# A gated cross-attention and LoRA block on one Trainium2 core: the program written anew, tile by tile

## What is computed

```python
def fake_quant(x, scale, zp):
    q = clip(round(x / scale + zp), 0, 255)
    return (q - zp) * scale
x = x + tanh(g_xattn) * (fake_quant(layernorm(x), s1, z1) @ fake_quant(ctx, s2, z2))   # per batch
h = layernorm(x)
logits = h @ Wr.T                              # 4 experts, the best 2 are kept
gates = softmax(logits of the best 2, else 0)
mid = einsum('tf,erf->ter', h, A)              # A: 4 experts x rank 16 x 2048
delta = sum_e gates[e] * (mid[e] @ B[e].T) * 4
x = x + tanh(g_ffn) * delta
```

## Time and profile before

| | |
|---|---|
| time, median of 3 runs | 423.1 us (422.08 to 425.37) |
| profiled execution | 423.39 us, span 421.7 us |
| TensorE matmul busy | 355.9 us, 84% of the span |
| VectorE busy | 314.9 us, 75% |
| ScalarE busy | 260.8 us, 62% |
| POOL busy | 85.6 us, 20% |
| HBM read, written | 51.42 MB, 16.78 MB |

### The profile page before, as it was taken

How to read it: one execution, slowest core, us unless ns; L and a number is a source line. 1 busy time by engine, 2 the same in 40 slices (tenths; PEclk the granted TensorE clock), 3 DMA queues, 4 the chain that set the end, 5 groups by cost and what they waited for, 6 DMA issues and landing times. The chain is left out here.

```text
span 421.7 us, 7130 instructions
## 1 busy us (share of the span) xinstructions
PE 355.9 (84%) x2352; PEld 207.1 (49%) x2352; DVE 314.9 (75%) x732; ACT 260.8 (62%) x240; POOL 85.6 (20%) x74
## 2 busy tenths in 40 slices
PE   0075569489898999989898999999999999999974
PEld 0032324265545454645555565656565656565552
DVE  2469994889877878787878777777777777676684
ACT  1757796578868585868777465656555565656150
POOL 1000000222222040403122222222313231314030
PEclk9999759779999999999999999999999999999986
DMA  4999980269474645465552322222322222312022
GB/s 143 331 400 426 427 371 2 99 209 307 185 234 133 210 145 189 181 184 173 195 203 101 100 103 101 99 99 99 99 99 99 99 99 99 102 50 101 0 101 100
DMA packets 22240, 68.51 MB, mean 162 GB/s; under 512 B 3204, under 2 KB 3716, under 8 KB 20100
## 3 DMA queue, kind: packets, MB, share of 16 engines
q1 hardware_dynamic: 22216, 68.20, 45.3%
HBM read 51.42 MB, written 16.78 MB: 162 GB/s over the span
## 5 line engine op out<-in xcount | busy, mean ns | idle before, releaser
L538 PE MATMUL ps_main<-q,q1T 128*128 128x512 f16 x928 | 212.1, 379 | 0.0
L538 PEld LDWEIGHTS ps_main<-q,q1T 128*128 128x128 f16 x928 | 87.7, 98 | 101.0 <-issue 7.0
L404 ACT ACTIVATE h_hi<-x,small_tile 128x1024 f16<-128x1024 f32 x32 | 39.4, 1233 | 61.6 <-DVE small_tile L825 61.6
L350 POOL TENSOR_TENSOR h_lo<-work,h_hi 128x1024 f16<-128x1024 f32 x31 | 66.7, 2151 | 46.1 <-ACT work L408 44.3
L809 DVE SCALAR_TENSOR_TENSOR x<-ps_main,small_tile,xt 128x512 f32<-128x512 f32 x60 | 44.7, 746 | 24.2 <-DMA out_x<-x 14.8
L787 DVE BATCH_NORM_STATS2 small_tile<-xt 128x6 f32<-128x512 f32 x64 | 40.7, 682 | 19.8 <-DMA xt<-in_x 19.8
L344 POOL TENSOR_TENSOR small_tile<-small_tile 128x1 f32<-128x1 f32 x16 | 8.8, 551 | 200.8 <-DVE small_tile L821 200.8
L390 ACT ACTIVATE x_byte<-xt,small_tile 128x1024 uint8<-128x1024 f32 x32 | 38.1, 1233 | 16.2 <-DVE small_tile L803 16.2
L814 DVE BATCH_NORM_STATS2 small_tile<-x 128x6 f32<-128x512 f32 x64 | 44.3, 692 | 1.7
L883 DVE TENSOR_TENSOR x<-ps_delta,x 128x512 f32<-128x512 f32 x64 | 42.3, 683 | 2.7 <-PE ps_delta L604 2.7
L383 ACT ACTIVATE ctx_stage<-ctx_stage,small_tile 128x1024 uint8<-128x1024 f32 x32 | 38.7, 1233 | 3.4 <-DMA ctx_stage<-in_ctx 3.4
(11 more groups left out here) (97 smaller groups left out, 367.8 us busy)
## 6 DMA issues: line engine op xcount, KB each, us to landing
xt<-in_x SPq DMA_DIRECT2D x32, 512.0 KB, 3.8
q<-in_ctx SPq DMA_DIRECT2D x16, 1024.0 KB, 18.0
ctx_stage<-in_ctx SPq DMA_DIRECT2D x32, 512.0 KB, 5.4
out_x<-x SPq DMA_DIRECT2D x64, 256.0 KB, 2.2
x<-in_L_ffn_A SPq DMA_DIRECT2D x1, 512.0 KB
x<-in_L_ffn_B SPq DMA_DIRECT2D x1, 512.0 KB, 14.9
small_tile<-in_L_xattn_x_scale SPq DMA_DIRECT2D x2, 0.5 KB, 4.0
small_tile<-in_L_xattn_x_zp SPq DMA_DIRECT2D x2, 0.5 KB, 4.3
```

The lines of the kernel that those rows point to most:

```text
L350: nc.gpsimd.tensor_tensor(h_lo[:, h, :], work[:, h, :], h_hi[:, h, :], ALU.subtract).then_inc(h_lo_ready, 1)
L404: nc.scalar.activation(h_hi[:, h, :], x1[:, b % 2, half(h)], ACT.Identity, bias=h_bias[:, :], scale=h_rstd[:, :]).then_inc(h_hi_ready, 1)
L538: mm = pe.matmul(acc[:, :], q1T[:, b % 2, k, :], q2[:, batch(b), k, cols(n)], start=(k == 0), stop=(k == KT - 1))
```

## The change

The same mathematics in a program written anew. In words:

- The host lays out A (one 128 x 1088 float32 array, turned) and B (128 x 2048, doubled), and joins six parameters in one array, which ScalarE's queue loads. The turning of A and B on TensorE and their splits in the load stage are gone. A gets a power-of-two scale per column (`largest_of_a`, `scales_of_a`, `powers_of_a`, `spread_scales`, `copy_scales`) and is split on POOL into two float16 parts in place of three bfloat16 ones, so that `mid_hi` has 136 columns and `mid_lo` 68; `rank_gates` multiplies the middle by the scales. `high_of_b` and `low_of_b` write B's two halves on VectorE.
- x lies in a ring of four tiles and x1 is written in place; loads of x wait for the store of four tiles before.
- In the load stage each row is added to four banks of tile 0 and, from row 4 on, to three of tile 1 (with the first four caught up). The tiles' scales and q1T of tiles 0 and 1 have new places; q1T of these two is copied on VectorE.
- Rows of batch 1 come whole, in two stages: rows 0 to 3 ahead of slot 4, then three per slot in slots 4 to 7. B's array lies in stage 1 first, A's in the x ring's fourth place.
- q1 is turned through the bank of the gates and copied at once (2048 columns); `scale_x` and `high_part` are one operation of 2048 columns; stores are 512 KB but for the last tile's.
- Both delta pairs of tile b-2 are in slot b; for the last tile the four banks are separate. Nothing is a loop any more.

The diff, cut to its core (buffers and banks; SyncE; POOL; ScalarE's order; TensorE; VectorE's order):

```diff
-        xt = sb("xt", [P, 2, D], F32)
-        x1 = sb("x1", [P, 2, D], F32)
+        xr = sb("xr", [P, RING, D], F32)
+        ctx_stage = sb("ctx_stage", [P, STAGES, N], F32)
         q1T = sb("q1T", [P, 2, KT, P], F16)
         lora_bT = sb("lora_bT", [P, N], F32R)
-        a_parts = sb("a_parts", [P, KT, 3, J], BF16)
+        a_parts = sb("a_parts", [P, KT, 2, J], F16)
...
+        first_banks = [ps_main + ps_delta, [ps_mid] + ps_turn + [ps_main[0]],
+                       [ps_main[1], ps_delta[0], ps_delta[1], ps_main[0]]]
         def product_bank(b, n):
...
+            def load_ctx(k):
+                wait(sp, ctx_coded, k - STAGES + 1)
+                if k == 1:
+                    sp.wait_ge(b_ready, 1)
+                sp.dma_start(ctx_stage[:, k % STAGES, :], ctx_pairs[(KT + k) // 2, k % 2, :, :]).then_inc(ctx_loaded[k % STAGES], 16)
...
+            load_x(0)
+            load_row(0)
+            load_row(1)
+            load_x(1)
+            for k in range(2, 12):
+                load_row(k)
+            load_x(2)
+            for k in range(12, KT):
+                load_row(k)
+            sp.dma_start(a_raw, lora_a).then_inc(a_loaded, 16)
+            sp.dma_start(b_raw, lora_b).then_inc(b_loaded, 16)
+            load_ctx(0)
+            sp.wait_ge(a_ready, 1)
+            load_x(3)
+            load_ctx(1)
+            load_ctx(2)
...
+            c = 3
+            for b in range(3, TILES):
+                if b == 3:
+                    store(0, range(2), HALF)
+                    load_x(4)
+                    todo = 2
+                elif b == 4:
+                    store(1, range(2), HALF)
+                    load_x(5)
+                    load_ctx(c)
+                    c += 1
+                    store(2, range(2), HALF)
+                    load_x(6)
+                    todo = 2
+                else:
+                    store(b - 2, range(2), HALF)
+                    if b + 2 < TILES:
+                        load_x(b + 2)
+                    todo = 3
+                for _ in range(todo):
+                    if c < KT:
+                        load_ctx(c)
+                        c += 1
+            store(LAST - 1, range(2), HALF)
+            store(LAST, range(NB), BANK)
...
+            def split_a():
+                a_view = a_raw.rearrange("p (k j) -> p k j", j=J)
+                pool.wait_ge(a_loaded, 16)
+                pool.wait_ge(a_scale_ready, 1)
+                nc.gpsimd.tensor_tensor(a_view, a_view, scales[:, 1, :].unsqueeze(1).to_broadcast([P, KT, J]), ALU.mult).then_inc(a_part_step, 1)
+                pool.wait_ge(a_part_step, 1)
+                nc.gpsimd.tensor_copy(a_parts[:, :, 0, :], a_view).then_inc(a_part_step, 1)
+                pool.wait_ge(a_part_step, 2)
+                nc.gpsimd.tensor_tensor(a_parts[:, :, 1, :], a_view, a_parts[:, :, 0, :], ALU.subtract).then_inc(a_ready, 1)
+            power_x(0)
+            power_x(1)
+            power_x(2)
+            split_a()
+            power_h(0)
+            low_part(0, 0)
+            power_h(1)
+            low_part(0, 1)
+            power_x(3)
...
+            scale_x(0)
+            scale_row(0)
+            scale_row(1)
+            scale_row(2)
+            scale_x(1)
+            for k in range(3, 13):
                 scale_row(k)
...
+            scale_x(2)
+            scale_row(13)
+            scale_row(14)
+            scale_row(15)
+            copy_q1T(2)
...
+            scale_ctx(1)
+            copy_loT(0)
...
+            scale_x(3)
+            high_part(1)
+            normal_half(1, 0)
+            normal_half(1, 1)
+            copy_q1T(3)
...
+            copy_hiT(2, 1)
+            scale_ctx(3)
+            copy_loT(2)
+            scale_x(4)
+            gate_exp(2)
+            copy_q1T(4)
+            c = 4
+            for b in range(4, TILES):
+                high_part(b - 1)
+                normal_half(b - 1, 0)
+                normal_half(b - 1, 1)
+                if c < KT:
+                    scale_ctx(c)
+                    c += 1
+                copy_hiT(b - 1, 0)
+                copy_hiT(b - 1, 1)
+                if b < LAST:
+                    scale_x(b + 1)
+                copy_loT(b - 1)
+                if b < LAST:
+                    copy_q1T(b + 1)
+                if c < KT:
+                    scale_ctx(c)
+                    c += 1
+                gate_exp(b - 1)
+                if c < KT:
+                    scale_ctx(c)
+                    c += 1
+            high_part(LAST)
+            copy_hiT(LAST, 0)
+            copy_hiT(LAST, 1)
+            copy_loT(LAST)
+            gate_exp(LAST)
...
+                    mm = pe.matmul(ps_mid[:, J:2 * J], hT[:, h, k, :], a_parts[:, kk, 0, :], start=False, stop=(kk == KT - 1))
...
+            def last_delta():
+                pe.wait_ge(gT_step, TILES)
+                pe.wait_ge(x1_ready, NB * TILES)
+                pe.wait_ge(out_ready, NB * LAST)
+                banks = ps_delta + ps_main
+                for n in range(2):
+                    pe.matmul(banks[n][:, :], gT_hi[:, :], lora_bT[:, cols(n)], start=True, stop=False)
+                pe.wait_ge(gT_ready, TILES)
+                for n in range(2):
+                    pe.matmul(banks[n][:, :], gT_lo[:, :], lora_bT[:, cols(n)], start=False, stop=True).then_inc(delta_done, 1)
+                for n in range(2, NB):
+                    pe.matmul(banks[n][:, :], gT_hi[:, :], lora_bT[:, cols(n)], start=True, stop=False)
+                    pe.matmul(banks[n][:, :], gT_lo[:, :], lora_bT[:, cols(n)], start=False, stop=True).then_inc(delta_done, 1)
...
+                for k in range(KT):
+                    if k == JOIN - 1:
+                        turn_q1(1, 0)
+                    if k == KT - 2:
+                        turn_q1(2, 0)
+                    pe.wait_ge(row_coded, k + 1)
+                    for n in range(NB):
+                        product(0, n, k, general)
+                    if k == JOIN:
+                        pe.wait_ge(q1T_ready, 2)
+                        for kk in range(k):
+                            for n in range(3):
+                                product(1, n, kk, general)
+                    if k >= JOIN:
+                        for n in range(3):
+                            product(1, n, k, general)
+                main(1, 3, general)
+                scales_of_a()
+                main(2, 0, general, 0, 8)
+                spread_scales()
+                main(2, 0, general, 8)
+                main(2, 1, general)
+                turn_hi(0)
+                main(2, 2, general, 0, 10)
+                high_and_turn_low(0)
+                main(2, 2, general, 10)
+                low(0)
+                main(2, 3, general, 0, 14)
+                turn_gate(0, 3)
+                main(2, 3, general, 14)
+                turn_q1(3, 1)
+                turn_hi(1)
+                main(3, 0, general, 0, 4)
+                delta(0, 0)
+                main(3, 0, general, 4)
+                delta(0, 2)
+                high_and_turn_low(1)
+                main(3, 1, general, 0, 8)
+                low(1)
+                main(3, 1, general, 8)
+                turn_hi(2)
+                main(3, 2, general, 0, 10)
+                turn_gate(1, 4)
+                high_and_turn_low(2)
+                main(3, 2, general, 10)
+                low(2)
+                main(3, 3, general, 0, 8)
+                delta(1, 0)
+                main(3, 3, general, 8, 14)
+                turn_gate(2, 4)
+                main(3, 3, general, 14)
+                delta(1, 2)
+                turn_q1(4, 3)
+                for b in range(4, TILES):
+                    if b == 4:
+                        main(b, 0, general)
+                        delta(b - 2, 0)
+                        main(b, 1, general)
+                        delta(b - 2, 2)
                     else:
+                        main(b, 0, general, 0, 4)
+                        delta(b - 2, 0)
+                        main(b, 0, general, 4)
+                        delta(b - 2, 2)
+                        main(b, 1, general)
+                    turn_hi(b - 1)
+                    main(b, 2, general, 0, 10)
+                    high_and_turn_low(b - 1)
+                    main(b, 2, general, 10)
+                    if b < LAST:
+                        turn_q1(b + 1, b - 1)
+                    low(b - 1)
+                    main(b, 3, general, 0, 14)
+                    turn_gate(b - 1, min(b + 2, TILES))
+                    main(b, 3, general, 14)
+                delta(LAST - 1, 0)
+                delta(LAST - 1, 2)
+                turn_hi(LAST)
+                high_and_turn_low(LAST)
+                low(LAST)
+                turn_gate(LAST, TILES)
+                last_delta()
...
+            def largest_of_a():
+                dve.wait_ge(a_loaded, 16)
```

(93 more changed lines are left out.)

1039 lines of the change are left out of this document (418 added, 621 removed).

## The result

The changed kernel takes **453.22 us** (median of 4 runs, 450.71 to 456.28); the kernel before, run beside it, 423.73 (422.08 to 425.37). Ratio 1.0699, 95% interval 1.062 to 1.0779: 7.0% slower. The prediction said 437.0 (413 to 449), slower at 0.70. The direction was right, the size was not: the time lies 4 us above the range. The profiled execution has a span of 451.6.

What follows compares the result with a forecast made beforehand. It took in-order engine queues to bound the kernel up to slot 7, then gapless TensorE: 147.7 to main(4,0), 105 for slots 4 to 7, 161.6 for slots 8 to 15, tail 21.9, sum 436.2, 437.9 with 1.7 outside; it said 437 (413 to 449).

Steps and rivals of the forecast that it cites:

- main(4,0) starts: Load stage through tile 3: main(4,0) starts at 147.7, where it was 142.3, so 5.4 later.
- slots 4 to 7: Slots with three whole rows each: 26 a slot, 27 for slot 4, 105 against 91.1, 13.9 more.
- slots 8 to 15: Slots without context rows: narrower middles bring 20.7 to 20.2 a slot, 161.6 in all, 3.8 less.
- tail: After main(15,3): 22.8 becomes 21.9, by 0.9 more for h_hi, 1.3 less for deltas, 0.5 less for middles.
- Load stage: First stage: row 15 coded at 62, 4.6 earlier; TensorE done at 63.5, not 73.06, with one bank more.
- the four chains: Load to loop: scaling A, bias_h(0) 78; load_ctx(1), low(0) 96.8; q1T(3), main(3,0) 114; tile 3, main(4,0) 147.7.
- the first two chains: Before the loop: A's scaling and POOL split to bias_h(0) at 78; B's split and load_ctx(1) to low(0) at 96.8.
- 25.1 at least: Slots 4 to 7: floor per slot of the chain through copy_q1T, second scale_ctx, code_ctx and gates, against 22.8.
- rival C: Slots 4 to 7: waits drop TensorE to 1.2 GHz, moving turn_q1 some 1.7; slots 27.7, total 447; chance 0.15.
- its 0.4: Slots 8 to 15: stats_h and the low part put the gate 0.4 past the fourteen matmuls that cover it.
- A: Whole kernel, faster: VectorE's work the only bound after the load, main(4,0) at 127, slots 25.1; 412.6; chance 0.14.
- B: Whole kernel, gains and losses cancel: chains some 5 shorter, main(4,0) at 142.3, slots 25.1; 425.5; chance 0.16.

Runs made afterwards that it cites:

- e4: Changed kernel with POOL computing power_h(0) ahead of the three operations that split A; 450.66 us, ratio 1.0619.
- e8: Changed kernel with ScalarE doing copy_loT(0) and gate_exp(0) ahead of scale_ctx(1), before the loop; 448.94 us, ratio 1.0597.
- e10: Changed kernel with high_of_b and low_of_b ahead of bias_h(0) in VectorE's queue; 449.01 us, ratio 1.0574.
- e14: The spread row order of e13 together with the edits of e3, e8 and e4; 422.92 us, ratio 1.0008.
- e15: On top of e14, the work on tiles 1 and 3 ahead of the loop ordered anew; 413.85 us, ratio 0.9758.
- experiment 2: Changed kernel with 22 added matmuls keeping TensorE busy before turn_gate in slots 4 to 7; 452.47 us, ratio 1.0642.
- e5: Changed kernel with SyncE issuing a slot's first context row ahead of the store and x load; 449.88 us, ratio 1.0578.
- e1: Changed kernel with VectorE's second code_ctx behind weigh instead of ahead of add_main(b,2), slots 4 to 7; 444.31 us, ratio 1.0464.
- e13: Against e9, a slot's three rows spread evenly over SyncE's, ScalarE's and VectorE's queues; 433.36 us, ratio 1.0241.
- e3: Changed kernel with add_delta(14,1) ahead of bias_h(15) in the tail; 449.97 us, ratio 1.0603.
- e17: On top of e15, SyncE issues a slot's third row between the store and the x load; 410.19 us, ratio 0.9674.
- e7: On top of e6, ScalarE does the exponential ahead of its second scale_ctx; 441.56 us, ratio 1.0407.
- e9: Changed kernel with two codings a slot deferred to the next, ScalarE's rows and exponential reordered, two rows issued before the store; 447.24 us, ratio 1.0529.
- run 31: Not a follow-up run: the words come from the sentence that float16 matmuls with 68 moving columns run 31 ns apart.
- e12: Changed kernel with the row order of e9 and the edits of e3, e8 and e4; 434.05 us, ratio 1.0234.
- e6: Changed kernel with the edits of e1 and e5 together; 437.47 us, ratio 1.0312.
- experiment 11: The experiment that ran e17: third row issued ahead of the x load, on top of e15; 410.19 us, ratio 0.9674.

## Why the prediction fell short

**The ledger.** Its four terms against the profiled execution:

| | predicted | measured | |
|---|---|---|---|
| main(4,0) starts | 147.7 | 154.08 | +6.4 |
| slots 4 to 7 | 105 | 113.7 | +8.7 |
| slots 8 to 15 | 161.6 | 158.2 | -3.4 |
| tail | 21.9 | 25.7 | +3.8 |
| span | 436.2 | 451.6 | +15.4 |

Every step went the way it was forecast in direction (head later, slots 4 to 7 the largest loss, slots 8 to 15 a gain), except the tail.

**Load stage: each small term a little low.** Parameters landed at 7.10, not 5.5; ScalarE's two standstills were 7.7 and 4.6, not 7 and 4.2. Row 15 was coded at 64.85 instead of 62, and TensorE was through with the rows, at the start of main(1,3), at 68.09 instead of 63.5. That is still ahead of the 73.06 of the earlier trace rows, with one bank more, so the regime was right. The gap of some 7 between constants and TensorE's program held (12.2 to 18.98).

**Head: the four chains were right, three durations weren't.** largest_of_a took 2.09 (said 1.2), high_of_b 2.34 (said 1.6), low_of_b 3.85 (said 2.5, bound 3.0). bias_h(0) came at 81.18 with VectorE idle 5.35 before it (said 78, some 6); low(0) at 100.64 after 7.93 (said 96.8, 8). POOL's split_a took 2.49 + 1.09 + 2.26 = 5.8, at the low end. The two B steps were not underpriced as work: both began while a POOL operation was running, and from that operation's end they took 1.1 and 2.15, less than the 1.6 and 2.5 of the forecast (see the last section). What the sum had at nothing is 1.3 and 1.7 of waiting beside POOL. Of the 6.4 by which main(4,0) came late, some 3 were there at the end of the load stage, 3.8 at low(0) and 4.3 at main(3,0) (118.28, said 114); tile 3 took 35.8 in place of 33.7. e4, e8 and e10 take the first two chains apart: 4.1, 5.2 and 7.5 at gate 0. The two waits themselves (6 and 8) were right, but e14 and e15 show what the forecast did not see: once they are gone, gates 0 to 3 still take 72 until, in one edit, x3's scale and tile 1's h are taken ahead of the gates of tile 0, and then 62. It read chains one at a time.

**Slots 4 to 7: the step that failed.** The prediction put it: "DMA is no bound: 3 rows, an x tile and a store, 5.2 MB in 25 us". It priced the chain at "25.1 at least", took 26 and, for slot 4, 27, and put two terms at nothing: the wait for a row's landing, and the low clock behind TensorE's wait, which it kept for rival C. Slot 6 shows both. From gate to gate (208.66 to 237.46) it took 28.8, and 25.1 + 2.03 (ScalarE's wait for the row at 230.56) + 1.8 (the clock, as in experiment 2) is 28.9. The bytes were right and the conclusion wrong: SyncE's queue is in order, so the row's load stood 11.9 behind the freeing of its stage. e5 bears the sum out: with its issue moved the landing waits are gone and the slots take 27.0 to 27.2, where 25.1 + 1.8 is 26.9. In the four slots the landings are 3.3 of the 8.7, and three slots at 26.9 in place of 26 another 2.7. Slot 4 was 28.8 long (154.08 to 182.9), not 27: its main(4,0) too ran in large part at the low clock, 4.95 from its start to the delta (154.08 to 159.03) where 3.46 is the full rate. The last 0.9 is not taken apart. The named chain (second scale_ctx behind copy_q1T, coding ahead of rank_gates) was real, as e1 and e13 show.

**Slots 8 to 15: mid_lo.** The prediction granted 0.16 a tile of a possible 0.48, since weight loads might set the pace. At 343.31 sixteen mid_lo start within 0.50, 31 ns apart, where before sixteen took 0.96: all of it was gained. The gate stayed covered, so its 0.4 was not lost. 158.2 / 8 = 19.8 a slot in place of 20.2 lies at the low end of the bounds, 19.7 to 20.8. The Trainium skill (TensorE: Matmul & The Clock Gate, Back-to-back issue gap) gives N / 2.4 + 2.5 ns for one isolated matmul, by which 68 columns are an estimated 30.8, and says that a stream with weight loads sustains about 81 ns at 128 columns. The first agrees with the 31 here. The second does not: eight transposes of 128 columns with eight loads start within 343.31 - 342.86 = 0.45, 56 ns each.

**Tail: a wait not seen.** The forecast costed the tail by durations and asked for each new order only what it saves. At 434.43 TensorE stood 4.95 for add_delta(14,1), with turn_hi(15) behind it at 435.88; e3 gave 2.4 back. Asking "what is queued behind this wait" once more would have found it.

**The rivals.** A (412.6, faster) did not happen. e17 comes near its number, 410.2, but by luck: main(4,0) starts at 137.6 there (A: 127), and the four slots take 227.18 - 137.56 = 89.6 (A: 100.4), two errors that cancel. What e17 does show is that VectorE, ScalarE and two stages are no bound at 25.1 a slot. B was missed by the same late chains. C came nearest: its mechanism is there, 1.8 a slot against the 1.7 that it gave, and its 151 + 111 for head and slots stands against 154.1 + 113.7. The argument against it, that the clock had stayed full in slots 3 to 7 of before, failed because TensorE's waits before the gates there were 0.2 and not 5 to 7.

## What to carry to other kernels

A queue taken in order turns *where an operation stands* into a cost of its own: the same instructions cost 451.6 and 409.1 here, and the span moved by 20.3 with the places of three rows and one exponential. Put work that comes in fixed portions (rows of a second input) evenly into gaps that an engine has anyway, and ask of each load not only its rate but when its queue lets it be issued. When a mended wait gives less than its size, look for the second entry to the same chain before calling it small: in slots 5 to 8 one repair gave 7.0, the other 2.7, both 12.0. Price a long wait of TensorE with the slow stretch behind it; and a wait that vanishes (e7, e9) is no gain until the next gate comes earlier.

## What the runs showed of the hardware

- With 68 moving columns and a 128x128 weight load each, float16 matmuls run 31 ns apart (sixteen in 0.50, at 343.31 in after): the loads stay hidden even there.
- VectorE and POOL took turns in some pairs of operations. high_of_b (128x2048 float32 to fp32r, both in SBUF) took 2.34 in after, 2.48 in e10 and 1.82 in e12, and each time it ended 1.07 to 1.08 after the end of the POOL operation that was running when it began (86.86, 77.36 and 80.80). low_of_b took 3.85, 3.06 and 3.96, and ended 2.14 to 2.15 after such a POOL operation. The other way round, POOL's cast and subtraction for A took 1.97 and 4.18 in e10, beside these two, where they take 1.09 and 2.26 in after. The timeline of e10:

```profile
74.87 2.49 POOL L310 TENSOR_TENSOR xr<-xr,scales 128x1088 f32<-128x1088 f32 x1 [19.39 <-DVE scales L785]
...
75.95 2.48 DVE L790 TENSOR_SCALAR lora_bT<-ctx_stage,small_tile 128x2048 fp32r<-128x2048 f32 x1
77.42 1.97 POOL L312 CAST a_parts<-xr 128x1088 f16<-128x1088 f32 x1
78.47 3.06 DVE L794 SCALAR_TENSOR_TENSOR lora_bT<-ctx_stage,small_tile,lora_bT 64x2048 fp32r<-64x2048 f32 x1
79.47 4.18 POOL L314 TENSOR_TENSOR a_parts<-xr,a_parts 128x1088 f16<-128x1088 f32 x1
```

And POOL's power, 0.55 as a rule, took 1.5 in four places of after, each time begun beside a VectorE operation of 2048 columns and ended 0.4 after it. In e12 a low_part took 3.11 in place of 2.13, begun beside high_of_b. The timelines of after and, below, of e12:

```profile
84.73 2.13 POOL L303 TENSOR_TENSOR h_lo<-work,h_hi 128x1024 f16<-128x1024 f32 x1 [3.59 <-ACT work L378]
...
85.60 2.34 DVE L790 TENSOR_SCALAR lora_bT<-ctx_stage,small_tile 128x2048 fp32r<-128x2048 f32 x1
...
86.82 1.54 POOL L297 TENSOR_TENSOR small_tile<-small_tile 128x1 f32<-128x1 f32 x1
```

```profile
80.75 3.11 POOL L307 TENSOR_TENSOR h_lo<-work,h_hi 128x1024 f16<-128x1024 f32 x1
```

That the one waits for the other's end is read from these times; no run has the B steps without POOL at work.
- How long a 1 MB row takes from issue to landing goes with what is issued around it: the median was 7.4 in after and 4.8, 5.5 and 5.3 in e5, e6 and e17, at the same traffic in all, and row 15 took 9.1 behind an x load and at most 5.7 ahead of one (experiment 11). That transfers in flight together share the engines is argued from the order of the issues; it was not measured by itself.
